# Windowed attention on a quarter of the TensorE array: 64x64 tiles, 48-partition operand stacks, and masks added by matmul

## The chip, the cores and the metric

The kernel runs on one core of one Trainium2 chip. The metric is the device time of one execution in microseconds. All times of the profile come from one profiled execution of the kernel before.

## The reference, cut to what matters

The input is x of 8 sequences, each 1024 positions by 256 features. A layer norm gives `xn`; then a transformer block with sliding-window attention and a gelu MLP, and an eight-expert layer that picks one expert for each position, are both applied to `xn` and added to x. The part that changes is the attention:

```
B, S, D, H, W, HD = (2, 1024, 256, 16, 64, 16)
scores = einsum('bnqhd,bnkhd->bhnqk', q, kc) * scale     # kc: own block of 64 keys and both neighbours
band = |i + W - j| <= W ; mask = band & valid            # invalid keys lie outside the sequence
scores = where(mask, scores, -1e9)
attn = softmax(scores); out = einsum('bhnqk,bnkhd->bnqhd', attn, vc)
```

So each block of 64 queries sees 192 keys: of the middle 64 all, of the left and the right 64 those inside the band.

## The kernel before, in words

**Loop.** The eight sequences are the turns of one loop, b = 0 to 7. Before it stands a prologue that loads and splits the weights and does the first part of sequence 0. Turn b does the attention of sequence b, its output projection (`b_stage`, L1186), the projections of sequence b+1 (`c2_stage`, L1055), and then the MLP of sequence b (`d_stage`, L1254) woven with the first scores and the expert layer of sequence b+1. The last turn has no b+1 parts. Each engine has its own program with the same order of stages, written out by hand; semaphores tie them together, and an engine that waits holds all that is queued behind on it.

**Projections and stacks.** `c2_stage` makes q and k of the next sequence in eight units. ScalarE writes the rounded part (`qk_h`, L918), VectorE the remainder (`qk_l`, L626). A score is computed in f16 as high x high plus high x low plus low x high. The three products lie in one contraction: for each head, 16 partitions of each of the three parts stand above each other, 48 partitions in all. SyncE builds these stacks (`stacks`, L269): it stores high and low parts to DRAM (`pair_dram`, L274; four stores of 512 KB), waits, and loads them back in 12 loads of 256 KB, each onto 16 partitions of `q_s` or `k_s` (L284), first q, then k. Two copies `q_s<-q_s` (L288) come last. `k_s` holds two heads above each other at partitions 0 and 64. `q_s` has a slot for each of the 16 heads with zeros where the other head's partitions are, so that a matmul over all 128 partitions picks one head.

**Scores twice.** The attention needs the row maxima before the exponentials. A step works on four heads (one group g of four) and one tile of 128 positions; there are 32 steps.
- `scores` (L1118) computes queries x keys in blocks of 64x192, eight matmuls a step into the two PSUM banks SB. VectorE adds the mask and takes the maxima (`maxima`, L703, four instructions a step at L713, each with a read of its accumulator).
- After each group `max_cols` transposes the maxima (L1139), VectorE scales them (L720), and SyncE writes them through DRAM into a row of `q_s` (L325, L331), where they join the contraction as one more row against a constant row of `k_s`.
- `scores_t` (L1142) computes keys x queries, 128x256, four matmuls a step into the two banks TB; ScalarE takes the exponentials (`exps`, L933, two of 512 columns a step at L943) into `prob`.
- GpSimd zeroes what lies outside the band (`band`, L435, two instructions a step at L440 and L445); in the steps 22 to 27 (`SHARED`) VectorE does the second one (L727).
- `values` (L1158) multiplies `prob` by v in f32 on four 32-column tiles, into the banks OB. `heads_out` (L946) copies them away.

**Order.** Scores run ahead of the exponentials by LEAD = 14 steps: six after units 5, 7, 9, 11, 13 and 15 of the 16 W1 units of the turn before (`W1_STEPS`), eight with its W2 tiles, and the 18 left in steps 1 to 18 of the attention. In those steps TensorE does half of `scores_t`, half of `scores`, the other halves, and then `values` of two steps before (`turn`, L1278). Steps 19 to 31 have `scores_t` and `values` alone. SB[0] also serves the ranks of the expert layer; the banks MB (6 and 7) serve the transposes.

**W1 units.** A unit (`w1_unit`, L1228) is six matmuls of 512 columns. ScalarE does the gelu (L989) and its rounded copy (L955), VectorE the remainder (`gelu_low`, L790). TB has two banks and `g32` two slots, so TensorE can run two units ahead of VectorE.

**GpSimd.** In its order: 32 times `band`; `residual` (L451, L453) of b+1; an inverse root (L386); `residual_attn` (L459); `fetch` (eight gathers at L490, then the add at L495); `send` (eight scatters of the expert layer's rows, L476); `residual_mlp` (L466, L468), which VectorE waits for before the first W2 tile. SyncE: the maxima's rows, loads of x and the residual, `store_res`, `stacks`, then the expert layer's tiles (`sorted_tiles`, L304), whose first load waits for the scatters.

Of the kernel before, what the change touches and what calls it, by code (L numbers as in the profile page):

```python
# [30 lines left out]
P = 128  # L31
W = 64
# [22 lines left out]
def build(nc, x, Wq, bq_c, Wk, bk_c, Wv, bv, Wo, bo, g1_c, b1, W1, c1_c, W2, c2, g2, b2, gateT, expT, b1_c, g1_row, out):  # L55
# [11 lines left out]
    SHARED = range(22, 28)  # L67
    XN_AT = 23
    WIN = 3 * W
    QW = 4 * W  # L70
# [9 lines left out]
    pair_dram = nc.dram_tensor("pair_dram", (2, 4, P, S), F16, kind="Internal").ap()  # L80
# [6 lines left out]
    assert len(W1_STEPS) + T == LEAD  # L87

# [4 lines left out]
    with ExitStack() as ctx:  # L93
# [8 lines left out]
        mask = sb("mask", [P, 3, WIN], BF16)  # L102
# [25 lines left out]
        pool2 = sb("pool2", [P, 3 * 4 * QW], F32)  # L128
        q_s = sb("q_s", [P, H, S + 2 * W], F16)
# [15 lines left out]
        keep = sb("keep", [P, 2 * W], BF16)  # L145
# [11 lines left out]
        prob = pool2[:, :].rearrange("p (s h q) -> p s h q", s=3, h=4)  # L157
# [15 lines left out]
        SB, TB, OB, MB = bank[0:2], bank[2:4], bank[4:6], bank[6:8]  # L173
# [27 lines left out]
        NSTACK = 2 * 2 * 3 + 2  # L201
        stack = count("stack", 16 * NSTACK)
        pair_st = count("pair_st", 16 * 4)
# [4 lines left out]
        ST_ps, ex_done, masked, pv = (count(n, k) for n, k in (("ST_ps", 2 * STEPS), ("exp_done", 2 * STEPS), ("masked", 2 * STEPS - len(SHARED)), ("pv", STEPS)))  # L208
        masked_v = count("masked_v", len(SHARED))
        oT_ev = count("oT_ev", 2 * G)  # L210
# [25 lines left out]
        def _(sp):  # L236
# [31 lines left out]

            def stacks(b):  # L269

                for qk in range(2):
                    for half, (src, done) in enumerate(((qk_h, qk_hi), (qk_l, qk_lo))):
                        sp.wait_ge(done.sem, done.at(b, 4 * qk + 4))
                        sp.dma_start(pair_dram[half, 2 * qk:2 * qk + 2].rearrange("o p s -> p o s"),  # L274
                                     src[:, 2 * qk:2 * qk + 2, :]).then_inc(pair_st.sem, 16)
                    sp.wait_ge(pair_st.sem, pair_st.at(b, 32 * (qk + 1)))

                    for a in range(2):
                        for slot in range(3):
                            low = slot == (1 if qk else 2)  # L280
                            src = pair_dram[int(low), 2 * qk:2 * qk + 2].rearrange("c (j a d) s -> a d (c j) s", a=2, d=HD)[a]
                            r = W * a + HD * slot
                            dst = k_s[r:r + HD, :, W:W + S] if qk else q_s[r:r + HD, a:H:2, W:W + S]
                            sp.dma_start(dst, src).then_inc(stack.sem, 16)  # L284

                for a in range(2):
                    r = W * a + 3 * HD
                    sp.dma_start(q_s[r:r + 1, a:H:2, W:W + S], q_s[r:r + 1, 1 - a:H:2, W:W + S]).then_inc(stack.sem, 16)  # L288
# [38 lines left out]
            def max_rows_in(b, g):  # L327
                sp.wait_ge(mx_st.sem, mx_st.at(b, 16 * (g + 1)))
                for a in range(2):
                    r = W * a + 3 * HD  # L330
                    sp.dma_start(q_s[r:r + 1, 4 * g + a:4 * g + 4:2, W:W + S],  # L331
                                 max_dram[g:g + 1, a::2, :]).then_inc(mrow.sem, 16)
# [40 lines left out]
        def _(pool):  # L373
# [29 lines left out]
            step(nc.gpsimd.memset(mask[:, :, :], 0.0))  # L403
# [7 lines left out]

            for a in range(2):
                part = mask[W * a:W * a + W, :, :]
                step(nc.gpsimd.affine_select(out=part, in_=part, compare_op=ALU.is_ge, fill=NEG, base=0,
                                             pattern=[[0, 3], [1, WIN]], channel_multiplier=-1))
                step(nc.gpsimd.affine_select(out=part, in_=part, compare_op=ALU.is_ge, fill=NEG, base=2 * W,
# [18 lines left out]
            def band(b, k):  # L435
# [6 lines left out]
                if k in SHARED:  # L442
                    return
# [917 lines left out]
```

## Time and profile before

| | us |
|---|---|
| time, median of 3 runs | 1560.16 (1558.44 to 1561.64) |
| span of the profiled execution | 1553.1 |
| TensorE matmul busy | 1240.9 (80%) |
| VectorE busy | 1071.5 (69%) |
| ScalarE busy | 739.8 (48%) |
| GpSimd busy | 739.9 (48%) |
| mean granted TensorE clock | 0.913 of 2.4 GHz |

The span runs from the first to the last instruction of the profiled execution; the time of a run holds a few microseconds more around it, here 7.1 between this span and the median. An engine's busy time counts overlapping instructions once. Weight loads of TensorE are a row of their own (PEld), since they run beside matmuls. In the profile a wait is told as "engine line waited for: us, times, longest". In a row of the timeline the bracket gives the idle time before the instruction and what ended it.

### The profile page before, as it was taken

The page shows a single profiled execution, that of the slowest core. Times are in us where ns is not written, and L with a number is a line of the kernel's source. Part 1 is how long each engine was busy: PE and PEld are TensorE (multiplying, and loading weights), DVE is VectorE, ACT ScalarE, POOL GpSimd, SP SyncE. Part 2 cuts the span into 40 slices and gives each one's busy share as a digit, 9 for nine tenths or more (in the row PEclk, how much of TensorE's full clock was granted, in tenths as well). Part 3 has the DMA queues.
Part 4 walks back from the last instruction along what each step waited for, and adds up shares of the span by engine and source line. Part 5 has one row for each costly group of instructions (what it writes and reads, how often), then busy time and mean ns, then how long its engine had stood idle before and what let it go on. Part 6 is the DMA issues. An engine that isn't in the chain of part 4 may idle for free.

```text
span 1553.1 us, 34323 instructions
## 1 busy us (share of the span) xinstructions
PE 1240.9 (80%) x10696; PEld 714.8 (46%) x10696; DVE 1071.5 (69%) x3743; ACT 739.8 (48%) x1356; POOL 739.9 (48%) x749
## 2 busy tenths in 40 slices
PE   0648885999678985999859997689858898599967
PEld 0424452735346353654527454373535535265435
DVE  8656775777757775867757677576766676587565
ACT  1305744366543744447443565426544374445642
POOL 6443745156531766037550474406752177504661
PEclk9959997999989997989979899798988899799979
DMA  7463056220733119130462206422082212912010
GB/s 237 92 139 118 3 117 122 76 92 29 144 79 100 57 69 166 50 112 13 108 131 69 99 8 145 91 83 83 33 156 75 88 57 74 162 48 94 2 28 28
DMA packets 89647, 135.00 MB, mean 87 GB/s; under 512 B 10209, under 2 KB 62305, under 8 KB 87393
## 3 DMA queue, kind: packets, MB, share of 16 engines
q1 hardware_dynamic: 83328, 115.91, 30.0%
q0 software_dynamic: 6144, 16.79, 4.4%
q8 instruction: 107, 1.75, 0.5%
q14 instruction: 68, 0.55, 0.1%
HBM read 74.47 MB, written 59.90 MB: 87 GB/s over the span
## 4 chain that ended last, share of the span: by engine, by line
PE 49%; DMA 17%; issue 11%; POOL 8%; DVE 8%; SPq 3%; ACT 3%; DVEq 0%; POOLq 0%; ACTq 0%
DMA pair_dram<-pool 9%; PE bank L1132 8%; PE bank L1035 8%; PE bank L1154 8%; PE bank L1036 7%; PE bank L1038 7%; PE bank L1181 6%; DMA q_s<-q_s 5%; DVE xn L604 2%; SPq L284 2%; DMA ys_dram<-xn 2%; PE bank L1102 2%; POOL x_sb L453 2%; POOL x_sb L451 2%; POOL rs L386 2%
## 5 line engine op out<-in xcount | busy, mean ns | idle before, releaser
L713 DVE CUSTOM_DVE_ANT_0 bank<-bank,mask 128x192 f32<-128x192 f32 x1024 | 337.3, 388 | 199.1 <-PE bank L1132 195.1
L943 ACT ACTIVATE pool<-bank 128x512 f32<-128x512 f32 x512 | 293.0, 597 | 118.9 <-PE bank L1154 113.2
L1132 PE MATMUL bank<-k_s,q_s 128*64 128x192 f16 x2048 | 175.3, 269 | 144.1 <-DMA q_s<-q_s 141.2
L440 POOL TENSOR_SCALAR_AFFINE_SELECT pool<-pool 128x512 f32<-128x512 f32 x256 | 172.2, 675 | 194.1 <-ACT pool L943 193.4
L1154 PE MATMUL bank<-q_s,k_s 128*128 128x256 f16 x1024 | 199.3, 290 | 28.7 <-issue 21.3
L389 POOL TENSOR_TENSOR rs<-ve,neghalf 128x1 f32<-128x1 f32 x64 | 36.9, 577 | 384.8 <-DVE ve L776 384.8
L1132 PEld LDWEIGHTS bank<-k_s,q_s 128*64 128x64 f16 x2048 | 77.8, 113 | 250.1 <-issue 226.9
L1181 PE MATMUL bank<-pool,v_a 128*32 128x256 f32 (+2 forms) x2560 | 161.1, 345 | 19.9 <-DVE pool L727 8.6
L989 ACT ACTIVATE pool<-bank,c1c 128x512 f32<-128x512 f32 x128 | 87.8, 686 | 169.5 <-PE bank L1038 132.5
L790 DVE TENSOR_TENSOR pool<-pool 128x512 f16<-128x512 f32 x128 | 106.7, 839 | 63.3 <-ACT pool L955 62.2
L713 DVE DVE_READ_ACCUMULATOR2_ANT m_sb<- 128x1 f32 x1024 | 144.6, 141 | 0.3
L931 ACT ACTIVATE xn<-bank 128x256 f32<-128x256 f32 x120 | 46.1, 384 | 202.6 <-PE bank L1038 195.0
L1154 PEld LDWEIGHTS bank<-q_s,k_s 128*128 128x128 f16 x1024 | 67.0, 100 | 144.5 <-ACT pool L943 76.4
L445 POOL TENSOR_SCALAR_AFFINE_SELECT pool<-pool 128x512 f32<-128x512 f32 x208 | 132.5, 637 | 0.0
L1036 PE MATMUL bank<-w_l,pool 128*128 128x256 f16 x512 | 115.3, 273 | 0.0
L1035 PE MATMUL bank<-w_h,pool 128*128 128x256 f16 x512 | 115.2, 273 | 0.0
L1035 PE MATMUL bank<-tr_h,w_h 128*128 128x512 f16 x256 | 105.3, 411 | 11.5 <-ACT pool L989 11.5
L1036 PE MATMUL bank<-tr_l,w_h 128*128 128x512 f16 x256 | 104.2, 407 | 0.0
L918 ACT ACTIVATE pool<-bank,bqk 128x512 f16<-128x512 f32 x64 | 44.0, 687 | 93.1 <-PE bank L1038 93.1
L1181 PEld LDWEIGHTS bank<-pool,v_a 128*32 128x32 f32 x2560 | 53.0, 110 | 71.8 <-issue 27.2
L955 ACT ACTIVATE pool<-pool 128x512 f16<-128x512 f32 x128 | 80.6, 630 | 4.5
L1038 PE MATMUL bank<-tr_h,w_l 128*128 128x512 f16 x256 | 80.8, 399 | 0.0
(149 smaller groups left out, 2511.1 us busy)
## 6 DMA issues: line engine op xcount, KB each, us to landing
pair_dram<-pool SPq DMA_DIRECT2D x32, 512.0 KB, 7.6
xn<-xs_dram SPq DMA_DIRECT2D x40, 384.0 KB, 3.7
ys_dram<-xn SPq DMA_DIRECT2D x120, 128.0 KB, 1.7
q_s<-pair_dram SPq DMA_DIRECT2D x48, 256.0 KB
k_s<-pair_dram SPq DMA_DIRECT2D x48, 256.0 KB
x_sb<-in_L_attn_x SPq DMA_DIRECT2D x8, 1024.0 KB, 5.7
res_dram<-x_sb SPq DMA_DIRECT2D x8, 1024.0 KB, 4.8
res_r<-res_dram SPq DMA_DIRECT2D x8, 1024.0 KB, 7.4
```

Source lines behind the costliest of these rows:

```text
L440: nc.gpsimd.affine_select(out=p, in_=p, compare_op=ALU.is_ge, fill=0.0, base=0, pattern=[[0, 4], [1, 2 * W]], channel_multiplier=-1).then_ ...
L445: nc.gpsimd.affine_select(out=p, in_=p, compare_op=ALU.is_ge, fill=0.0, base=0, pattern=[[0, 4], [-1, 2 * W]], channel_multiplier=1).then_ ...
L713: ins = nc.vector.tensor_tensor_reduce(out=SB[u % 2][:, i * WIN:i * WIN + WIN], in0=SB[u % 2][:, i * WIN:i * WIN + WIN], in1=mask[:, v, :] ...
L790: nc.vector.tensor_tensor(gL[hf][:, c, :], g32[:, u % 2, :], gH[hf][:, c, :], ALU.subtract).then_inc(g_lo.sem, 1)
L943: nc.scalar.activation(prob[:, (k + 2) % 3, 2 * pu:2 * pu + 2, :], TB[u % 2][:, :].rearrange("p (h q) -> p h q", h=2), ACT.Exp, scale=EXP_ ...
L989: nc.scalar.activation(g32[:, u % 2, :], TB[u % 2][:, :], ACT.Gelu_apprx_tanh, bias=c1c[:, c:c + 1], scale=1.0 / WS).then_inc(gel.sem, 1)
L1035: nc.tensor.matmul(dst, lh[c], rh[c], start=start and c == 0, stop=False)
L1036: nc.tensor.matmul(dst, lh[c], rl[c], start=False, stop=False)
L1038: mm = nc.tensor.matmul(dst, ll[c], rh[c], start=False, stop=stop and c == n - 1)
L1132: mm = nc.tensor.matmul(SB[u % 2][W * bl:W * bl + W, i * WIN:i * WIN + WIN], q_s[:, h, W + w0:2 * W + w0], k_s[:, h // 2, w0:w0 + WIN], st ...
L1154: mm = nc.tensor.matmul(TB[u % 2][:, i * QW:i * QW + QW], k_s[:, h // 2, W + t * P:W + t * P + P], q_s[:, h, t * P:t * P + QW], start=True ...
L1181: mm = nc.tensor.matmul(OB[hf][32 * hl:32 * hl + 32, a - hf * HALF:z - hf * HALF], v_a[:, t, 4 * g + hl, :], prob[:, (k + 2) % 3, hl, q0:q ...
```

## The change

Six edits go together.
- **Stacks.** The columns of Wq, bq, Wk and bk are permuted on the host so that in a projection's output partition d * 8 + head holds feature d of a head. The stores write `pair_dram` in the stack's order, in 12 stores of 256 KB; the loads take a whole stack of 48 partitions for four head slots at once, 8 loads of 384 KB. The projections' units come in the order q and k of heads 0 to 7, then q and k of heads 8 to 15, and SyncE stores unit pair i and then loads pair i-1. `scores` waits at step 0 for the stacks of heads 0 to 7 alone and at step 16 for the others. `q_s` has the form of `k_s`; the `q_s<-q_s` copies go.
- **64x64 tiles.** `scores` and `scores_t` both compute blocks of 64x192 over one head's 48 or 64 partitions, eight matmuls each a step, ordered over both row halves (the parity of the head) and both column halves.
- **Masks by matmul.** Four matmuls more for `scores` and four for `scores_t` a step, each of 256 columns, add -1e30 outside the band by an identity. GpSimd's and VectorE's `band` go, and VectorE's maxima are two plain reductions of 2x192 columns a step.
- **Values.** `values` computes over the 64 keys of a block, on eight 64x32 tiles, the upper and the lower keys of a tile into different banks (OB, and 6 and 7); VectorE adds the two (`heads_sum`, two a group). The exponentials are of 384 columns.
- **Banks.** MB is now SB, so that `max_cols` waits for all scores issued so far, and the next scores (at `MAX_STEPS`) wait for VectorE's copy.
- **Order.** A step issues all of `scores_t`, waiting for both exponentials of the step before, and then all of `scores`, waiting for both maxima of the step before.

```diff
-    SHARED = range(22, 28)
+    MAX_STEPS = [LEAD - T + 3] + [T * g + MAX_AT - 1 + LEAD for g in range(G - 2)]
-        SB, TB, OB, MB = bank[0:2], bank[2:4], bank[4:6], bank[6:8]
+        SB, TB, OB = bank[0:2], bank[2:4], bank[4:6]
+        MB = SB
+        PV = (bank[4:6], bank[6:8])
...
+            def pair_stores(b, i):
+                c, qk = divmod(i, 2)
+                for src, done, slots in ((qk_h, qk_hi, (0, 2 if qk else 1)), (qk_l, qk_lo, (1 if qk else 2,))):
+                    sp.wait_ge(done.sem, done.at(b, 2 * i + 2))
+                    for slot in slots:
+                        sp.dma_start(pair_dram[c, qk, :, :, slot, :, :].rearrange("j a d s -> d (j a) s"),
+                                     src[:, 2 * qk + c, :]).then_inc(pair_st[i % 2].sem, 16)
+            def stack_loads(b, i):
+                c, qk = divmod(i, 2)
+                sp.wait_ge(pair_st[i % 2].sem, pair_st[i % 2].at(b, 48 * (i // 2 + 1)))
+                dst = k_s if qk else q_s
+                for a in range(2):
+                    sp.dma_start(dst[W * a:W * a + KW, 4 * c:4 * c + 4, W:W + S],
+                                 pair_dram[c, qk, :, a, :, :, :].rearrange("j o d s -> (o d) j s")).then_inc(stack[c].sem, 16)
             def stacks(b):
+                pair_stores(b, 0)
+                for i in range(1, 4):
+                    pair_stores(b, i)
+                    stack_loads(b, i - 1)
+                stack_loads(b, 3)
...
             def maxima(b, j):
+                for n, par in enumerate((1, 0)):
+                    dve.wait_ge(S_ps.sem, S_ps.at(b, 2 * j + n + 1))
                     dve.sem_inc(passed, 1)
+                    nc.vector.tensor_reduce(m_sb[:, 4 * g + par:4 * g + 4:2, t],
+                                            SB[par][:, 0:2 * WIN].rearrange("p (h c) -> p h c", h=2), AX.X, ALU.max).then_inc(mx.sem, 1)
+            def heads_sum(b, g, hf):
+                dve.wait_ge(oT_ev.sem, oT_ev.at(b, 2 * g + hf + 1))
+                o = oT[:, g, hf * HALF:hf * HALF + HALF]
+                nc.vector.tensor_tensor(o, PV[1][hf][:, :], o, ALU.add).then_inc(oT_sum.sem, 1)
...
+            def mask_mm(out, n, t, par):
+                r = slice(W * par, W * par + W)
+                band = mask[r, edge(2 * t + n), :, :].unsqueeze(1).broadcast_to([W, 2, 2, W])
+                dst = out[W * n:W * n + W, 0:2 * WIN].rearrange("p (h c k) -> p h c k", h=2, c=3)[:, :, 0::2, :]
+                return nc.tensor.matmul(dst, ident16[r, :], band, start=False, stop=True, skip_group_check=True)
+            def scores(b, j, first=False):
+                for par in (1, 0):
+                    scores_wait(b, j, par, first)
+                t = j % T
+                for i in range(2):
+                    for n in range(2):
+                        for par in (1, 0):
+                            score_mm(SB[par], n, j, par, i)
+                for n in range(2):
+                    for par in (1, 0):
+                        mm = mask_mm(SB[par], n, t, par)
+                        if n == 1:
+                            mm.then_inc(S_ps.sem, 1)
...
             def turn(b, last):
                 for k in range(STEPS + LAG):
                     if k % T == MAX_AT and k < 3 * T:
-                        max_cols(b, k // T + 1)
-                    for pu in range(2):
-                        if k < STEPS:
-                            scores_t(b, k, pu)
-                        if 1 <= k and k - 1 + LEAD < STEPS:
-                            scores(b, k - 1 + LEAD, half=pu)
+                        max_cols(b, k // T + 1, min(k - 1 + LEAD, STEPS))
+                    if k < STEPS:
+                        scores_t(b, k)
+                    if 1 <= k and k - 1 + LEAD < STEPS:
+                        scores(b, k - 1 + LEAD)
```

`scores_wait` waits for `mx.at(b, u - 1)` of both parities before the first matmul, and at `MAX_STEPS` for `mT_ev`. `scores_t` has the same form with q and k exchanged and waits for `ex_done.at(b, 2 * k)`. On GpSimd the inverse root and `residual` of b+1 now come first in the turn.

## Rows read from the trace of the kernel before

**Rows 1.** Waits of the whole run, TensorE's for the stacks: us, times, longest.
```profile
PE bank L1132 <- DMA q_s<-q_s: 141.2, 8, 22.6
```

**Rows 2.** Waits from 560 to 640 us, inside turn 2.
```profile
PE bank L1132 <- DMA q_s<-q_s: 17.1, 1, 17.1
```

**Rows 3.** Timeline of SyncE's issues in turn 1: start us, us, what.
```profile
392.15 5.24 SPq L274 DMA_DIRECT2D pair_dram<-pool  x2
420.11 2.69 SPq L284 DMA_DIRECT2D k_s<-pair_dram  x6
422.84 1.38 SPq L288 DMA_DIRECT2D q_s<-q_s  x2
```

**Rows 4.** Windows of turn 1: busy us of each engine, then PEclk, DMA share, GB/s.
```profile
416.00:418.00 2.00, 1.31 (x7) 0.39 (x4) 2.00 (x1) 0.10 (x1) 2.00 (x1) 1.00 1.00 278
424.00:432.00 8.00, 0.00 (x0) 0.00 (x0) 0.76 (x1) 0.34 (x1) 6.16 (x8) 0.61 1.09 124
435.00:439.00 4.00, 3.68 (x15) 1.55 (x16) 1.37 (x8) 0.11 (x1) 3.92 (x2) 0.50 0.42 148
```

**Rows 5.** Timeline from 413 to 437 us of turn 1, GpSimd and who it holds.
```profile
414.47 4.50 POOL L495 TENSOR_TENSOR res_r<-res_r,x_sb 128x2048 f32<-128x2048 f32 x1 [10.12 <-DMA x_sb<-ys_dram,pos_y]
...
420.97 0.39 PE L1035 MATMUL bank<-tr_h,w_h 128*128 128x512 f16 x1 [3.66 <-ACT pool L989]
...
431.79 4.52 POOL L466 TENSOR_TENSOR pool<-pool,bc 128x2048 f32<-128x2048 f32 x1
...
435.32 0.85 PE L1132 MATMUL bank<-k_s,q_s 128*64 128x192 f16 x8 [12.88 <-DMA q_s<-q_s]
...
436.39 4.51 POOL L468 TENSOR_TENSOR pool<-pool,bc 128x2048 f32<-128x2048 f32 x1
```

**Rows 6.** Timeline of attention step 13 of turn 2, and the next step's start.
```profile
522.68 0.39 PE L1154 MATMUL bank<-q_s,k_s 128*128 128x256 f16 x2
...
523.00 0.36 PE L1132 MATMUL bank<-k_s,q_s 128*64 128x192 f16 x4
...
523.11 1.21 ACT L943 ACTIVATE pool<-bank 128x512 f32<-128x512 f32 x2 [0.58 <-PE bank L1154]
...
523.29 0.39 PE L1154 MATMUL bank<-q_s,k_s 128*128 128x256 f16 x2
...
523.55 0.37 DVE L713 CUSTOM_DVE_ANT_0 bank<-bank,mask 128x192 f32<-128x192 f32 x1 [0.42 <-PE bank L1132]
...
523.90 0.64 PE L1181 MATMUL bank<-pool,v_a 128*32 128x192 f32 x16
...
524.47 0.39 PE L1154 MATMUL bank<-q_s,k_s 128*128 128x256 f16 x2
```

**Rows 7.** Costliest groups by form: busy us, mean ns, idle before.
```profile
L943 ACT ACTIVATE pool<-bank 128x512 f32<-128x512 f32 x512 | 293.0, 597 | 118.9 <-PE bank L1154 113.2
L1154 PE MATMUL bank<-q_s,k_s 128*128 128x256 f16 x1024 | 199.3, 290 | 28.7 <-issue 21.3 <-ACT pool L943 4.1 <-DMA q_s<-max_dram 1.3
L972 ACT ACTIVATE pool<-bank 128x256 f32<-128x256 f32 x64 | 24.6, 385 | 65.1 <-PE bank L1216 49.8 <-PE bank L1208 15.3
L691 DVE TENSOR_REDUCE tef<-own 128x15 f32<-128x105 f32 x8 | 2.1, 263 | 0.3
L666 DVE TENSOR_REDUCE tiles<-oh 128x8 f32<-128x64 f32 x8 | 1.8, 220 | 0.3
```

**Rows 8.** Timeline of turn 1: steps without scores, first, 28th and last.
```profile
351.81 0.61 PE L1154 MATMUL bank<-q_s,k_s 128*128 128x256 f16 x4
...
365.38 1.09 ACT L943 ACTIVATE pool<-bank 128x512 f32<-128x512 f32 x2 [0.51 <-PE bank L1154]
...
369.61 0.61 PE L1154 MATMUL bank<-q_s,k_s 128*128 128x256 f16 x4
```

**Rows 9.** Timeline of turn 1: VectorE's copy of the maxima.
```profile
353.25 0.28 DVE L720 TENSOR_SCALAR mT<-bank 32x128 f16<-32x128 f32 x1 [0.88 <-PE bank L1139]
```

**Rows 10.** Window inside those steps, columns as in rows 4.
```profile
362.00:365.00 3.00, 1.70 (x21) 0.68 (x22) 3.00 (x8) 2.35 (x5) 0.65 (x1) 1.00 0.02 5
```

More of the change, by code:

```diff
@@ L267, in load_x @@
                 sp.dma_start(x_sb[:, :, :], x_v[b]).then_inc(x_in.sem, 16)
-            def stacks(b):
[L271 to L288, printed above, removed]
@@ L497, in turn @@
             def turn(b, last):
-                for k in range(STEPS):
-                    band(b, k)
-                    if k == XN_AT - 1 and not last:
-                        rstd(b + 1, 0, ve0, rs0)
                 if not last:
+                    rstd(b + 1, 0, ve0, rs0)
                     residual(b + 1)
@@ L838, in turn @@
                         xn_low(b + 1, k - (STEPS - 4))
+                heads_sum(b, G - 1, 1)
                 b_stage(b)
@@ L1116, in sorted_expert, with edge, score_mm @@
                 mm.then_inc(y_ps.sem, 1)
-            def scores(b, j, first=False, half=None):
+            def edge(n):
+                return 0 if n == 0 else 2 if n == 2 * T - 1 else 1
+            def score_mm(out, n, j, par, i):
                 g, t = divmod(j, T)
-                if j == 0 and not half:
-                    pe.wait_ge(route.sem, route.at(b, 6))
-                    pe.wait_ge(stack.sem, stack.at(b, 16 * NSTACK))
-                for pu in range(2) if half is None else (half,):
-                    u = 2 * j + pu
-                    if not first or u >= 2:
-                        pe.wait_ge(mx.sem, mx.at(b, u - 1))
-                    for i in range(2):
-                        h = 4 * g + 2 * pu + i
-                        for bl in range(2):
-                            w0 = (2 * t + bl) * W
-                            mm = nc.tensor.matmul(SB[u % 2][W * bl:W * bl + W, i * WIN:i * WIN + WIN],
-                                                  q_s[:, h, W + w0:2 * W + w0], k_s[:, h // 2, w0:w0 + WIN],
-                                                  start=True, stop=True)
-                    mm.then_inc(S_ps.sem, 1)
@@ new lines, in values @@
+                    pe.sem_inc(passed, 1)
+                pieces = []
+                for a in range(2):
+                    blk = 2 * t + a
+                    for hf in range(2):
+                        lo, hi = max(blk - 1, T * hf, 0), min(blk + 2, T * hf + T)
+                        if lo < hi:
+                            pieces.append((a, hf, blk, lo, hi))
+                for hl in range(4):
+                    for a, hf, blk, lo, hi in pieces:
+                        first = blk in (0, 1) if hf == 0 else blk in (T - 1, T)
+                        last = blk in (T - 1, T) if hf == 0 else blk in (2 * T - 2, 2 * T - 1)
+                        c = (lo - blk + 1) * W
+                        r = slice(W * a, W * a + W)
+                        mm = nc.tensor.matmul(PV[a][hf][32 * hl:32 * hl + 32, (lo - T * hf) * W:(hi - T * hf) * W],
+                                              v_a[r, t, 4 * g + hl, :], prob[r, (k + 2) % 3, hl, c:c + (hi - lo) * W],
```

194 lines of the change are left out of this document (99 added, 95 removed).

## The prediction

> **What bounds the kernel now.** I read the waits of the whole run first, then the same list turn by turn, then SyncE's issues and the windows around the largest wait, then single steps of the attention. The largest wait of TensorE that nothing else covers is the one for the operand stacks: 141.2 us in 8 waits [rows 1]. The longest, 22.6 us, is the prologue's; the seven in the turns sum to 118.6 us, each like the 17.1 us of turn 2 [rows 2]. It stands at the first scores of the next sequence, in the middle of the W1 units. SyncE issues the k loads only at 420.11 us and the copies behind them at 422.84 us [rows 3], and TensorE does nothing in that window, while the queues move 124 GB/s at full share [rows 4]. After the wait the clock is at 0.5, which is 1.2 GHz, for about 4 us [rows 4].
>
> In the attention each step with scores takes 524.47 - 522.68 = 1.79 us, and TensorE follows itself without a gap [rows 6]. Of that only part is columns. Two `scores_t` matmuls of 256 columns take 0.21 us at 2.4 GHz, and the next group starts 0.32 us after them; the four of `scores`, two tiles side by side, take 0.16 us and hold 0.29 us. So a change of tile form costs about 0.12 us, five times a step. `values` holds 0.57 us, 0.45 us without its change. The 12 steps without scores take (369.61 - 351.81) / 12 = 1.48 us [rows 8].
>
> **The change part by part.**
>
> *TensorE in the attention.* If all four 64x64 tiles run side by side, `scores_t` is two waves of 192 columns and one of 256, 0.27 us, `scores` the same, `values` 0.45 x 192/256 = 0.34 us, and two changes of form are left: 1.12 us in place of 1.79 us. TensorE stops being the bound. What is late next is the way through the banks, since `scores` now waits for both maxima of the step before and `scores_t` for both exponentials.
>
> *Loop of the maxima.* From the first `scores` matmul to VectorE's start 0.55 us pass now [rows 6]. The mask wave starts 0.08 us later than today's last matmul and is 0.03 us longer: 0.66 us. A reduction grows by 43 ns for 41 columns [rows 7], so 384 columns take 220 + 320 x 1.05 = 556 ns. Two in a row should overlap as two exponentials do (1.09 us for two of 0.597 us [rows 8, 7]), so 1.02 us. For the way back I take 0.15 us, between the 0.04 us from TensorE's end to ScalarE's start and the 0.19 us to VectorE's [rows 6]. Sum 1.83 us against 1.79 us: 18 steps cost 0.7 us a turn. The bounds are 1.7 us (return 0.05 us, mask wave free) and 2.07 us (no overlap, and 0.3 us back through the added semaphore instructions).
>
> *Loop of the exponentials.* An exponential of 384 columns is 385 + 128 x 212/256 = 491 ns [rows 7], the pair 0.88 us. From `scores_t` to ScalarE 0.43 us pass now [rows 6], 0.09 us more with the mask wave; with the same 0.15 us back, 1.55 us. That is 0.07 us more than now, over 12 steps 0.8 us a turn. The bounds are 1.45 and 1.75 us.
>
> *The shared banks.* At steps 4 and 12 the transpose of the maxima stands between two scores: 0.29 us for the transpose, as for a matmul of twice its columns [rows 7], 0.19 us to VectorE, 0.28 us for the copy [rows 9]; 0.76 us each, 1.5 us a turn. In the W2 tiles one such wait is left, 0.5 us in seven turns: 3.5 us. It could be nothing, or 0.9 us each.
>
> *Band and sums.* GpSimd's 64 selections a turn ran beside the rest and are worth nothing; where `values` waited for them or for VectorE's share, that is inside the 1.48 us. `heads_sum` fits into VectorE's 0.7 us of waiting in a step. The last one stands ahead of the projection, and the last `values` no longer waits for GpSimd: I take zero for the two together (bounds 0.7 us a turn either way). The attention thus costs 0.7 + 0.8 + 1.5 = 3.0 us a turn, **24 us** over eight, with bounds of -12 and +70 us.
>
> *The stacks.* Stores grow from 2 to 3 MB, loads stay at 3 MB, issues go from 18 to 20, but the first scores need only the first half, and it goes first. In turn 1 the store that waits for the low part of four units is issued by 392.15 + 5.24 = 397.4 us [rows 3]; after the change the low part of two is enough, so I start there. Behind it stand 1.8 MB of stores at up to 278 GB/s, 1.6 MB of loads, 1 MB of gathers. The new loads go to 48 partitions, three times as many as the old; at the old loads' 124 GB/s [rows 4], the slow end, all has landed after 23 us, at 420 us. The wait began at 435.32 - 12.88 = 422.4 us [rows 5]. So the wait goes: **-118.6 us**, with 1 us a turn left for late landings, **+7 us** (bounds 0 and 21). The cold start behind it goes too: at half clock the 3.68 us of matmuls [rows 4] would take some 2.2, so 1.5 us a turn, **-10.5 us**. The prologue's wait I cost at nothing (bound -22.6 us [rows 1]), because its expert tiles then wait for GpSimd's scatters. If the second half is late, sixteen steps cover it; SyncE's later start on the expert tiles is covered as long as the scatters, behind which GpSimd goes on at 431.79 us [rows 5], are what they wait for.
>
> The Trainium skill (SBUF — State Buffer, Door 1: The DMA port swizzle) says that 16 partitions reach four of 16 ports and 48 reach eight. The full DMA share at 124 GB/s agrees with that for the old loads; by the rule the new ones would be faster and the 7 us would be nothing.
>
> *What the wait had hidden.* GpSimd's long adds hold VectorE where both of its inputs are in SBUF: during the one of 4.50 us at 414.47 us TensorE waited 3.66 us for the gelu behind VectorE [rows 5]. The two of `residual_mlp`, from 431.79 to 440.90 us, lie in the stack wait now. Without it they fall into the W1 units: 2 x 3.7 us in seven turns, **+52 us** (bounds 0 and 63). That add stood ahead of the stack wait in turn 1, 3.66 + 12.88 us together, and inside it in turn 2, whose one wait of 17.1 us is as long [rows 5, 2]. I take the six other turns like turn 2: 6 x 3.7 = **+22 us** (bounds 0 and 27).
>
> **Sum.** -118.6 - 10.5 + 7 + 52 + 22 + 24 + 3.5 = -20.6 us. The profiled span of 1553.1 us becomes 1532.5; this execution stands 7.1 us below the median of the runs, so the forecast is **1540 us**.
>
> **The rivals.**
>
> *The way through the banks is dearer (slower).* Place: the 30 steps of each attention. If the reductions don't overlap and the semaphores cost 0.1 us more each way, the loops are 2.07 and 1.75 us: 18 x 0.24 + 12 x 0.2 = 6.7 us a turn, 54 us, 1594 us. It decides once the steps are 0.09 us longer than I count (20.6 / 8 / 30). For it: today each half step has its own bank and waits for the one two before, and that slack goes. Against it: both engines get less work. Chance 0.14.
>
> The Trainium skill (TensorEngine Tiling (Array Packing), PSUM Bottleneck) warns that tiling speeds up the array and not the emptying of the banks. That is this rival's side; by the rule alone nothing of the 0.67 us on TensorE arrives, as in my sum.
>
> *The row halves take turns.* Then the change doesn't do what it says: two waves become four, 0.27 us more in each loop, 30 x 0.27 x 8 = 65 us, 1605 us. No row shows two row halves; the column halves do overlap [rows 6]. Chance 0.09.
>
> *The clock falls.* TensorE is busy half of each step without scores. At the half clock these are 0.27 us longer, 12 x 0.27 x 8 = 26 us, 1566 us. Against it: with 1.70 busy of 3.00 us the granted clock stayed at 1.00, 2.4 GHz [rows 10]. Chance 0.05.
>
> *The stack wait stays,* because six megabytes in small pieces take longer. Then the adds stay hidden as well: 1560 + 24 + 3.5 = 1588 us. Chance 0.04.
>
> *The adds don't bite.* With the gathers landing earlier or the adds in gaps of VectorE, the 74 us are in part free: between 1466 and 1515 us. Chance 0.13.
>
> **How the numbers follow.** My forecast has 0.55, its own range from its inner bounds is 1510 to 1572. Two in ten may fall outside: I leave out the lower half of the last rival and the worst of the row halves, and take 1497 to 1598 us. About 0.2%, 3 us, is what can be told from no change. Of my forecast's chance 0.49 is faster, 0.04 is the same, 0.02 slower; the last rival is faster, the others slower with 0.02 of them the same. Faster 0.62, the same 0.06, slower 0.32.
>
> **What would show it.** In the profile after: no wait of TensorE for a stack over 3 us inside a turn; two waits of 3 to 4 us for gelu during L466 and L468's successors, and the first expert tile about 7 us earlier in the turn; steps with scores of 1.83 us with TensorE idle for 0.7 us, without scores 1.55 us; reductions of about 556 ns; the first matmuls of `scores` on all four tiles within some 20 ns. I am wrong if these steps are over 1.92 us, if a second matmul on the other row half starts a wave late, if the granted clock in the attention is 0.5, or if the adds run without holding VectorE.

## The result, and the profile after

The changed kernel takes 1593.4 us (median; 1592.2 to 1594.9) where the kernel before takes 1559.3: a ratio of 1.0226 (95% interval 1.0202 to 1.025). The forecast was 1540 us; the changed kernel is 2.3% slower than the kernel before. Its profiled span is 1592.2 us, 39.1 us over the span before.

The first fence has lines of the page: busy time, the instruction queue, and the costliest groups (busy us, mean ns, idle before them).

```profile
PE 1217.2 (76%) x15816; PEld 737.0 (46%) x15816; DVE 1016.4 (64%) x2223; ACT 672.5 (42%) x1356; POOL 440.3 (28%) x286
...
q8 instruction: 147, 2.41, 0.7%
...
L702 DVE TENSOR_REDUCE m_sb<-bank 128x2 f32<-128x384 f32 x512 | 262.5, 553 | 205.2 <-PE bank L1135 202.8
L932 ACT ACTIVATE pool<-bank 128x384 f32<-128x384 f32 x512 | 223.2, 488 | 251.2 <-PE bank L1135 251.2
L777 DVE TENSOR_TENSOR pool<-pool 128x512 f16<-128x512 f32 x128 | 152.1, 1196 | 84.4 <-ACT pool L946 66.8
L1228 PE MATMUL bank<-pool,v_a 64*32 64x192 f32 (+2 forms) x4608 | 170.3, 336 | 23.4 <-issue 22.4
```

The instruction queue of the kernel before stood at less:

```profile
q8 instruction: 107, 1.75, 0.5%
```

A reduction takes 553 ns and an exponential 488 ns, as counted (556 and 491). No row of the waits names a stack any more; the 141.2 us of [rows 1] are gone. New are a mean of 1196 ns for `gelu_low` (L777), and 22.4 us for which `values` (L1228) waited for nothing that the profile shows. The next fence is the timeline of one step and the start of the next, the counterpart of [rows 6].

```profile
530.84 0.36 PE L1119 MATMUL bank<-k_s,q_s 48*64 48x192 f16 x8 [0.44 <-DVE m_sb L702]
...
531.00 0.31 PE L1135 MATMUL bank<-mask,ident 64*64 64x256 bf16 x4
...
531.25 0.59 PE L1228 MATMUL bank<-pool,v_a 64*32 64x192 f32 x24
531.46 1.02 DVE L702 TENSOR_REDUCE m_sb<-bank 128x2 f32<-128x384 f32 x2 [0.77 <-PE bank L1135]
...
532.28 0.87 ACT L932 ACTIVATE pool<-bank 128x384 f32<-128x384 f32 x2 [0.97 <-PE bank L1135]
...
532.63 0.56 PE L1119 MATMUL bank<-k_s,q_s 48*64 48x192 f16 x8 [0.39 <-DVE m_sb L702]
```

In the `scores` at 530.84 us four matmuls start within 0.01 us of each other, the next four 0.11 us later, and the masks 0.16 us after the first: so four tiles do run side by side, the two row halves among them. From one `scores` to the next 532.63 - 530.84 = 1.79 us pass, as before the change. Now read step 8 of the same turn:

```profile
518.88 0.54 PE L1228 MATMUL bank<-pool,v_a 64*32 64x192 f32 x11
519.10 1.02 DVE L702 TENSOR_REDUCE m_sb<-bank 128x2 f32<-128x384 f32 x2 [0.17 <-PE bank L1135]
521.45 0.14 PEld L1228 LDWEIGHTS bank<-pool,v_a 64*32 64x32 f32 x5 [2.41 <-issue]
521.46 0.52 PE L1228 MATMUL bank<-pool,v_a 64*32 64x192 f32 x5 [2.04 <-issue]
```

TensorE stops in the middle of `values`, after 11 of 16 matmuls, though their operands were there for the first. Such a step takes 4.0 to 5.7 us in turns 1 to 6.

The difference by stages, from the first exponential of each turn, the first transpose of `b_stage`, the first gelu, and the first expert tile in the two timelines; sums over all turns, us:

| stage | before | after | difference | forecast |
|---|---|---|---|---|
| prologue | 136.9 | 132.8 | -4.1 | 0 |
| attention | 442.5 | 498.7 | +56.2 | +24 |
| `b_stage`, `c2_stage` | 298.6 | 315.4 | +16.8 | 0 |
| W1 units to the first expert tile | 301.9 | 267.3 | -34.6 | -48.1 |
| W2 tiles, end of the last turn | 373.2 | 378.1 | +4.9 | +3.5 |

They sum to the spans' difference of 39.1 us but for rounding. (The -48.1 are -118.6 - 10.5 + 7 + 52 + 22.) Against the forecast of -20.6 us the attention is off by 32 us, `b_stage` with `c2_stage` by 17, the W1 stage by 13.5, and the prologue by -4.

### The profile page after: what moved, and what is told of

The parts are those of the page before. It is cut to its first block, busy times and chain, and to the rows that moved or that the text cites. A ratio compares the mean times of both kernels' runs of the same rounds, so it can differ in the third digit from the quotient of the medians.

```text
span 1592.2 us, 42888 instructions
## 1 busy us (share of the span) xinstructions
PE 1217.2 (76%) x15816; PEld 737.0 (46%) x15816; DVE 1016.4 (64%) x2223; ACT 672.5 (42%) x1356; POOL 440.3 (28%) x286
## 3 DMA queue, kind: packets, MB, share of 16 engines
q8 instruction: 147, 2.41, 0.7%
## 4 chain that ended last, share of the span: by engine, by line
issue 65%; POOL 16%; PE 9%; DVE 9%; ACT 1%; POOLq 0%; another core or an unknown queue 0%; DVEq 0%; ACTq 0%
POOL xs_dram L472 4%; PE bank L1029 3%; PE bank L1026 2%; PE bank L1027 2%; POOL pool L464 2%; POOL rs L396 2%; POOL x_sb L449 2%; POOL x_sb L447 2%; POOL pool L462 2%; POOL rs L393 2%; DVE xn L597 1%; DVE oh L637 1%; PE bank L1035 1%; DVE pool L777 1%; DVE pool L619 1%
## 5 line engine op out<-in xcount | busy, mean ns | idle before, releaser
L702 DVE TENSOR_REDUCE m_sb<-bank 128x2 f32<-128x384 f32 x512 | 262.5, 553 | 205.2 <-PE bank L1135 202.8
L932 ACT ACTIVATE pool<-bank 128x384 f32<-128x384 f32 x512 | 223.2, 488 | 251.2 <-PE bank L1135 251.2
L777 DVE TENSOR_TENSOR pool<-pool 128x512 f16<-128x512 f32 x128 | 152.1, 1196 | 84.4 <-ACT pool L946 66.8
L1228 PE MATMUL bank<-pool,v_a 64*32 64x192 f32 (+2 forms) x4608 | 170.3, 336 | 23.4 <-issue 22.4
L1119 PE MATMUL bank<-k_s,q_s 48*64 48x192 f16 x2048 | 105.3, 281 | 98.9 <-DVE m_sb L702 78.6
L1135 PE MATMUL bank<-mask,ident 64*64 64x256 bf16 x2048 | 172.4, 308 | 0.0
L1127 PE MATMUL bank<-q_s,k_s 64*64 64x192 f16 x2048 | 103.4, 281 | 78.0 <-ACT pool L932 48.6
L1119 PEld LDWEIGHTS bank<-k_s,q_s 48*64 48x64 f16 x2048 | 47.2, 113 | 169.5 <-issue 169.2
L1228 PEld LDWEIGHTS bank<-pool,v_a 64*32 64x32 f32 x4608 | 69.5, 111 | 82.8 <-issue 81.5
L472 POOL DMA_INDIRECT xs_dram<-xn,pos x64 | 64.8, 1013 | 55.9 <-DVE pos L677 36.7
```

Source lines behind the costliest of these rows:

```text
L472: nc.gpsimd.indirect_dma_start(out=xs_dram[:, :], out_offset=bass.IndirectOffsetOnAxis(ap=pos[:, t:t + 1], axis=0), in_=xn[:, t, :], in_of ...
L702: nc.vector.tensor_reduce(m_sb[:, 4 * g + par:4 * g + 4:2, t], SB[par][:, 0:2 * WIN].rearrange("p (h c) -> p h c", h=2), AX.X, ALU.max).th ...
L777: nc.vector.tensor_tensor(gL[hf][:, c, :], g32[:, u % 2, :], gH[hf][:, c, :], ALU.subtract).then_inc(g_lo.sem, 1)
L932: nc.scalar.activation(prob[:, (k + 2) % 3, par::2, :], TB[par][:, 0:2 * WIN].rearrange("p (h q) -> p h q", h=2), ACT.Exp, scale=EXP_SCALE ...
L1119: return nc.tensor.matmul(out[W * n:W * n + W, i * WIN:i * WIN + WIN], q_s[r, h, q:q + W], k_s[r, h, q - W:q + 2 * W], start=i == 0, stop= ...
L1127: return nc.tensor.matmul(out[W * n:W * n + W, i * WIN:i * WIN + WIN], k_s[r, h, p:p + W], q_s[r, h, p - W:p + 2 * W], start=i == 0, stop= ...
```

## The experiments

Each ratio is against the kernel before on the same chip, so ratios are compared, 1% being about 15.6 us. The edits are cut to the lines that matter. The stacks alone, the two kernels with GpSimd's operations cut and the pad on TensorE ran on one chip (kernel before: 1560.9 us), the loads moved, the pad on ScalarE and the operations moved on a second (1549.1), the others on a third (1550.9 and 1548.5); the first pair's chip isn't on record (1559.3).

The chips differ in more than that. In the traces of the first chip and in that of the changed kernel ScalarE has waits without a releaser, which the profile puts down to "issue" or "remote" and to no instruction of the program, in the W1 stage and in `c2_stage`. In the changed kernel they are these:

```profile
ACT pool L980 <- remote: 21.8, 7, 5.4
ACT pool L908 <- issue: 10.5, 12, 1.5
```

In the ten traces of the other two chips there is none at these lines, whatever the edit. So a difference of some 1% between runs on different chips can be the chip's.

**The stacks alone.** In the kernel before, `pair_stores`, `stack_loads`, the new order of units and the two waits for halves replace the old ones; the two resets of the maxima's row go behind the first stores. The host doesn't permute Wq and Wk, so the heads' values are mixed up while all work is done.

```
+ dst = k_s[r, 4 * c:4 * c + 4, W:W + S] if qk else q_s[r, 8 * c + a:8 * c + 8:2, W:W + S]
- pe.wait_ge(stack.sem, stack.at(b, 16 * NSTACK))
+ pe.wait_ge(stack[0].sem, stack[0].at(b, 96))
```

> The kernel before with the new stores and loads of the stacks alone (48-partition loads, units in the new order, the first scores wait for the first half); tiles, masks and band as before. Theory A (the stacks give what the prediction counted, and the loss lies in the tiled attention): 1559 - 118.6 - 10.5 + 7 + 74 = about 1511 us, no wait for a stack over 3 us inside a turn, attention steps as before (1.79 us, 12 steps without scores 17.8 to 18.7 us). Theory B (the stacks' own traffic costs what it gains): 1545 us or more, with a wait for a stack left or the W1 stage as long as before.

Measured 0.9799 (0.9772 to 0.9825), 1531 us. No wait for a stack is left, and the attention steps are those of before. So the two halves of the change go opposite ways: the stacks give 2.0%, the tiles cost 1.0226 - 0.9799 = 4.3%, about 66 us. The gain is 31 us, between the 48 of theory A and the 14 or less of theory B.

**GpSimd's operations cut.** Two kernels, the changed one and the stacks alone:

```
- nc.gpsimd.tensor_tensor(n1[:, :, :], n1[:, :, :], bc[:, 4:5, :].broadcast_to([P, T, D]), ALU.mult)
+ nc.gpsimd.tensor_tensor(n1[:, 0, 0:8], n1[:, 0, 0:8], bc[:, 4, 0:8], ALU.mult)
```

> The changed kernel with GpSimd's three long operations in the W1 stage (the add after the fetch and the two of residual_mlp) cut to 8 elements a row; the rest of these sums is left out. Theory C (GpSimd's long operations hold VectorE longer than predicted, about 3 us at the one-hot row and 4.5 us at each of two gelu_low, and the cold clock follows from these waits): 12 us in each of seven turns, 1593 - 84 = about 1509 us. Rival (other work is late next, the scatters or the routing): a gain under 40 us, 1553 us or more.

> The stacks alone, and GpSimd's three long operations cut as well. If the adds bite as predicted, 74 us under the run with the stacks alone: about 1437 us. If the stack wait only hid other late work, less than 30 us under it.

Measured 0.9734 (0.9713 to 0.9754) and 0.9417 (0.9392 to 0.9442): 4.9% and 3.8% less than with the operations, 77 and 60 us where 84 and 74 were expected. In the seven W1 stages it is 63 us (267.3 to 204.2) and 54 us (263.9 to 210.0). The timeline of the changed kernel, turn 2, shows what they do:

```profile
602.83 4.50 POOL L491 TENSOR_TENSOR res_r<-res_r,x_sb 128x2048 f32<-128x2048 f32 x1 [7.69 <-DMA x_sb<-ys_dram,pos_y]
...
604.27 3.14 DVE L637 TENSOR_TENSOR oh<-sc,mx 128x64 f32<-128x64 f32 x1
...
608.66 0.19 PE L1079 MATMUL bank<-oh,before 128*128 128x72 f16 x1 [3.32 <-DVE oh L648]
...
621.13 0.69 ACT L980 ACTIVATE pool<-bank,c1c 128x512 f32<-128x512 f32 x1 [3.83 <-remote]
...
622.51 10.18 DVE L777 TENSOR_TENSOR pool<-pool 128x512 f16<-128x512 f32 x2 [3.55 <-issue]
622.72 4.52 POOL L462 TENSOR_TENSOR pool<-pool,bc 128x2048 f32<-128x2048 f32 x1
...
627.31 4.83 POOL L464 TENSOR_TENSOR pool<-pool,bc 128x2048 f32<-128x2048 f32 x1
...
633.78 0.54 PE L1119 MATMUL bank<-k_s,q_s 48*64 48x192 f16 x8 [6.30 <-DVE m_sb L702]
```

The add after the fetch stretches a VectorE operation of 64 columns to 3.14 us and TensorE waits 3.32 us for the one-hot rows. The other two make two `gelu_low` last 10.18 us, and behind them stands the maximum that frees the bank of the next `scores`: 6.30 us of wait for TensorE, while ScalarE waits 2.55 and 3.56 us ahead of two gelus. So the price comes not as two gelu waits alone, but as a held VectorE with everything behind it.

**The same operations moved.** They are cut by tile and put between GpSimd's operations of the W2 tiles; the sends go first.

```
- residual_mlp(b)
+ for t in range(2): residual_mlp(b, t); residual_y(b, t)
  for t in range(T):
      rstd(b, 2, ve2, rs2, t)
+     if t + 2 < T: residual_mlp(b, t + 2); residual_y(b, t + 2)
```

> The stacks alone, with GpSimd's three long operations of the W1 stage cut into eight tiles each and moved between its tile operations of the W2 stage; the sends go ahead of them. Theory C: VectorE is no longer held in the W1 stage, and in the W2 stage it has slack of 20%: 30 to 60 us under the run with the stacks alone, 1470 to 1500 us. Rival (held by small pieces just the same, or GpSimd's rstd behind them comes late for f_out): within 15 us of 1531.

> The changed kernel with the same cut and move of GpSimd's three operations. Theory C: 40 to 75 us under it, 1518 to 1553 us, and about 50 to 60 us over the run that has the stacks alone with this same cut, since the tiled attention costs the same in both. Rival (the tiled attention only loses against the adds' order): within 25 us of that run.

Measured 0.9147 (0.9117 to 0.9177) with the stacks alone, 1418 us where before takes 1549, and 0.960 (0.9564 to 0.9635) with the whole change. Both gains are over 6%, more than forecast (1470 to 1500 and 1518 to 1553 us) and more than with the operations cut. The W1 stage takes 23.9 and 23.8 us a turn where the kernel before has 43.1; the W2 tiles take some of it back (316.9 to 337.2 us with the whole change). The sends don't explain why moving gives more than cutting: the first starts 5.5 us after the turn's first gelu in both (6.1 to 8.3 us in the changed kernel). In the cut form of the changed kernel ScalarE still waits 61 us ahead of its gelus in seven turns, in the moved form 23, and these runs were on different chips; how much is the chip's is not shown. The tiles' price, measured on one chip here, is as before, 4.5% (72 us by the medians, 50 to 60 expected).

**TensorE's code moved by 128 instructions.**

```
+ for _ in range(128):
+     pe.sem_inc(passed, 1)
  with pe.Fori(0, NB - 1) as b:
```

> The changed kernel with 128 semaphore instructions on TensorE between the prologue and the loop; nothing in the loop differs, but its code stands 128 instructions further on. Theory D (TensorE waits for the next block of its instructions, of which it has 46% more a turn than before): the long step of 4 to 5.7 us, step 8 in turns 1 to 6, moves by one or two steps (some 87 instructions are one step), and those of the last turn move as well; the time may change by up to 15 us either way. Rival (the wait is for data, or for the 2 MB of loads issued two steps earlier): the long step stays step 8, and the time is the same within 3 us.

Measured 1.0365. The first exponential comes at 152.39 instead of 132.81 us, so the 128 instructions put it off by 19.6 us; from there to the end 1459.6 us pass, as in the changed kernel (1459.4). But step 8 is a plain step now (1.8 us), and the long ones are steps 1 (2.9 to 3.4 us in turns 1 to 6), 10 (up to 3.9 us) and 30 (2.9 to 3.1 us in most turns). Two rows of turn 2, TensorE's timeline:

```profile
528.87 0.53 PE L1127 MATMUL bank<-q_s,k_s 64*64 64x192 f16 x8 [2.15 <-issue]
...
548.41 0.36 PE L1119 MATMUL bank<-k_s,q_s 48*64 48x192 f16 x8 [2.19 <-issue]
```

The waits belong to places in the code, and not to one step's data. 2.41 MB in 147 packets is 16 KB each; the queue carried 107 before. Around step 8 of the changed kernel's turn 2 (513 to 521 us) the queues carry one such packet among 2 MB of data (packets, MB, share of 16 engines):

```profile
q1 hardware_dynamic: 1185, 2.07, 74.3%
q8 instruction: 1, 0.02, 0.8%
```

The Trainium skill (Runtime: NRT & Kernel Launch, Instruction fetch mechanics) says that instructions are fetched in blocks of 16 KiB while the block before runs, and that this is mostly hidden. The packet size agrees; that it is hidden holds for most blocks here, but not in step 8, by 2 us.

The trace has the start of each packet of this queue. In turn 2 one starts at 518.93 us, and `values` goes on at 521.46, 2.53 us later. It is so every time: in the attention of the changed kernel 78 such packets start, and the nine waits of TensorE over 1 us for which the profile names nothing (1.1 to 2.8 us, behind the first microsecond of each turn) end 2.3 to 2.9 us after the start of one. With the pad there are 18 such waits, ending 2.2 to 2.7 us after a packet; the attention of the kernel before has 44 packets and no such wait.

**The data beside it moved.** The loads of x and of the residual go behind the second pair of max rows.

```
  max_rows(b, 1)
+ max_rows(b, 2)
  load_x(b + 1); load_res(b)
- for g in range(2, G): max_rows(b, g)
+ max_rows(b, 3)
```

> The changed kernel with the loads of x and of the residual (2 MB) issued after the second pair of max rows, some ten steps later. Theory D1 (a block of TensorE's instructions comes late when its packet meets the data): step 8 of turns 1 to 6 falls from 4.0 to 5.7 us to under 2.5 us, and a long step may appear near steps 17 to 20, where the loads run now; 10 to 18 us less. Theory D2 (the block is late by itself, whatever the queues carry): step 8 stays over 4 us, time the same within 4 us.

Measured 1.0206 (1.0138 to 1.0274). Step 8 is 1.78 to 1.84 us in turns 1 to 6, and step 17, which had 1.8 us, takes 3.6 to 5.3 us; there the loads (issued at 529.85 us in turn 2) now run:

```profile
537.98 0.27 PE L1135 MATMUL bank<-mask,ident 64*64 64x256 bf16 x1 [2.06 <-issue]
```

D1 holds for the place of the wait: the eight waits over 1 us in this attention end 2.3 to 2.7 us after a packet too. But data beside it is not what every such wait needs. In the 3 us ahead of the packet the queues move 368 to 397 GB/s at step 8 of turns 1 to 6, and at most 5 GB/s at step 28 (0.5 to 0.8 us where the profile shows a wait) and at the waits of the last turn (up to 2.0 us). The gain of 10 to 18 us didn't come: the wait moved, the half clock in the attention rose from 135 to 230 us, and the attention is 15 us longer than the changed kernel's (513.9 and 498.7).

**ScalarE's code moved by 64 instructions** (the same edit ahead of ScalarE's loop).

> The changed kernel with 64 semaphore instructions on ScalarE ahead of its loop. Theory D: the wait of 2 to 5 us ahead of the seventh gelu of the W1 stage, for which the profile names no releaser (7 in all, 21.8 us), is ScalarE's own block of instructions and moves to another ScalarE instruction some 64 earlier. Rival (a semaphore, or TensorE's end, is late there): it stays at the seventh gelu. The time stays within 15 us.

Measured 1.0187 (1.0152 to 1.0222), 0.4% under the changed kernel with intervals that overlap. Waits of ScalarE for the gelu, first in the changed kernel, then in this one:

```profile
ACT pool L980 <- PE bank L1029: 60.5, 42, 4.8
ACT pool L980 <- DVE pool L777: 53.1, 18, 3.6
ACT pool L980 <- remote: 21.8, 7, 5.4
```

```profile
ACT pool L980 <- PE bank L1031: 63.2, 44, 5.8
ACT pool L980 <- DVE pool L777: 56.7, 18, 3.6
ACT L932 <- issue: 22.7, 7, 4.1
```

The 21.8 us without a releaser are gone, but that is no answer: this run was on the second chip, and there they are gone in the run with the loads moved too, whose ScalarE code is that of the changed kernel. What the pad did bring is the last line, seven waits of 2.4 to 4.1 us at the table load ahead of a turn's first exponential. No other trace has one over 1 us there. That ScalarE waits for its code there fits; for the 21.8 us the cause stays open. In the changed kernel they end 3.9 to 7.4 us after the last 16 KB packet of the instruction queue, not at one distance from it as TensorE's do.

**Fewer instructions.** Probabilities and v are rounded to fp16, so `values` needs half its matmuls.

```
- v_a = sb("v_a", [P, T, H, VW], F32)
+ v_a = sb("v_a", [P, T, H, VW], F16)
```

> The changed kernel with the probabilities and v kept in fp16 (they are rounded to it): values takes 288 weight loads and 288 matmuls a turn in place of 576 each, so TensorE's instructions fall from about 4350 to 3774 a turn and its time by 0.3 us a step. Theory D (in the attention TensorE waits for its blocks of instructions, not for its columns): the long steps grow rarer or shorter, 15 to 30 us less, 1563 to 1578 us by the first pair of medians. Rival (the steps are set by the way through the shared banks alone): steps stay 1.52 and 1.8 us and the long one stays, under 8 us less.

Measured 1.0354 (1.033 to 1.0379): slower than the changed kernel, by 25 us in the attention (523.9 and 498.7). The idle time ahead of `values` for nothing visible falls from 22.4 us to under 1 us, step 8 is as long as its neighbours in seven of the eight turns, and no wait over 1 us without a releaser is left in the attention:

```profile
L1228 PE MATMUL bank<-pool,v_a 64*32 64x192 f16 (+2 forms) x2304 | 89.8, 308 | 2.8 <-ACT pool L932 1.9
```

But the clock is at 0.5, 1.2 GHz, in nearly the whole attention (windows: busy of each engine, PEclk, DMA share, GB/s; turn 2):

```profile
513.00:543.00 30.00, 24.23 (x458) 11.95 (x454) 16.68 (x33) 12.97 (x30) 0.00 (x0) 0.50 0.21 73
543.00:565.00 22.00, 15.01 (x277) 7.59 (x277) 10.50 (x34) 12.32 (x28) 4.25 (x2) 0.50 0.01 3
```

Its steps take 1.80 us where they take 1.52 at 2.4 GHz, and 2.07 for 1.79. So half of my theory D was right and the forecast of the time wrong: the clock took back more than the waits had cost.

**The clock put back.** Zero-weight matmuls of 512 columns in every `values` (two a step).

```
+ nc.tensor.matmul(PV[1][pieces[-1][1]][0:W, :], q_s[:, 0, 0:W], w1_h[:, 0, 0:512],
+                  start=False, stop=False, skip_group_check=True)
```

> The changed kernel with fp16 probabilities and v, as before, and in every step of values two matmuls of 512 columns with zero weights, which add nothing but keep TensorE at work some 0.4 us more. Theory F (the run without them was slower because the clock fell to 0.5 in the whole attention, where TensorE had too little work): the clock stays at 1.0 in most steps, these take 1.52 and 1.8 us in place of 1.80 and 2.07, and with the long steps gone the time is 25 to 50 us under the run without the fillers, also 10 to 30 us under the changed kernel. Rival (the fp16 form itself is slower, or TensorE's extra work shows): the same or slower.

Measured 1.0196 (1.0144 to 1.0248), 1.6% under the run without them, though TensorE does more. In the second part of turn 2's attention:

```profile
545.00:568.00 23.00, 22.09 (x360) 10.04 (x359) 12.91 (x38) 14.67 (x34) 6.34 (x3) 1.00 0.01 3
```

Half clock in the attention: 82 us instead of 490. A long step is back (step 9, 3.1 to 4.3 us in six of turns 0 to 6), and with it most of what the clock gave.

**The order of halves.** The change's order undone: `scores_t` of one parity, `scores` of one parity, then the others.

```
+ for half in range(2):
+     scores_t(b, k, half)
+     scores(b, k - 1 + LEAD, only=1 - half)
```

> The changed kernel with the order of halves of before: transposed scores of one parity, scores of one parity, then the other two, each waiting for its own bank alone. Two of the four tiles run at a time, so TensorE needs some 0.3 us more a step. Theory E (the order of the change, all transposed scores and then all scores, makes each loop wait for both banks): steps without scores fall from 1.52 to about 1.2 us, those with scores from 1.78 to about 1.6 us, 30 to 55 us less in all if the blocks of instructions allow it. Theory D alone (instructions set the pace): steps 8 and 28 stay long, and less than 15 us are gained.

Measured 1.0158 (1.0112 to 1.0204), 0.7% under the changed kernel, the intervals touching, and on another chip; the attention is 7 us shorter (491.7 and 498.7). A plain step without scores takes 1.13 us, one with scores 1.35 to 1.6: the loops through the banks do shorten by up to 0.4 us. But steps of 2 to 3.5 us now stand between them, step 8 still takes 4.6 to 6.2 us in five turns, and the 12 steps from step 19 on take 19.7 to 22.3 us in turns 0 to 6 instead of 19.0 to 19.5. Both theories had a part, and neither number was met.

**Combinations.** Halves, fp16 and moved operations together; that with one filler a step; and the old tiles with the stacks, fp16 and moved operations.

> The tiled attention with the order of halves, fp16 probabilities and v, and GpSimd's operations in tiles. If order and instruction count were all that the tiles lost by, it comes within 15 us of the old attention with the same edits (about 1375 us). If not, it stays 40 us or more above it.

> Order of halves, fp16 values and GpSimd's operations in tiles, with one filler of 512 columns a step. Theory F: the half clock in the attention (350 of 437 us) goes, and 10 to 30 us with it. Rival: TensorE was the bound there at half clock because of its blocks of instructions; then the long steps come back and under 8 us are gained.

> The stacks alone with GpSimd's operations in tiles, and fp16 probabilities and v. In the old attention TensorE follows itself in the 18 steps with scores (1.79 us), so a values shorter by 0.3 us shows: 18 x 0.3 x 8 = 43 us, about 1375 us where the kernel before takes 1549. Rival (the exponentials are the bound just behind it): under 15 us.

Measured 0.9331 (0.9299 to 0.9363), 0.9348 (0.9321 to 0.9375) and 0.9015 (0.8988 to 0.9042). The filler halved the time at half clock in the attention (354 to 164 us) and gained nothing: the steps 2 to 6 take 2.3 to 3.1 us in most turns. The old tiles stay 3.2% ahead of the best form of the new ones. They gained 1.3% from fp16, 20 of the 43 us expected. At 1395 us (1394 to 1400) this is the fastest version, 10% under the kernel before; with f32 probabilities the fastest is the one of 1418 us.

## Why the prediction was wrong, point by point

**The stack wait** (-118.6 us) went as argued: no row is left of it, late landings cost nothing, and the prologue even gave 4 us. With GpSimd's operations moved the stage takes 23.9 instead of 43.1 us a turn, 135 us less in seven.

**What the wait had hidden** was the right mechanism, but "2 x 3.7 us" was not how it came: the second `gelu_low` is held as well, and so is the maximum behind it, with the bank of the next `scores`. In size the term was a little too large: with the one add that already bit the sum had 78 us, and cutting the operations takes 63 us out of the seven stages. What failed in this stage is a term that wasn't there. By the sum, the stage without the operations is 301.9 - 118.6 - 10.5 + 7 - 4 = 176 us; it takes 204.2 us with them cut. So about 28 us of other waits came in place of the stack's. With the operations moved, on another chip, it takes 166.3 us. In the changed kernel 21.8 us of ScalarE's waits have no releaser; the cause of these is open. The forecast that the first expert tile comes 7 us earlier held in four turns (the stage is 5 to 12 us shorter in turns 0, 1, 5 and 6); in turns 2 to 4 the stage took 42.3 us, as long as before.

**The attention** (+24 us) is where the sum broke, by 32 us. Its parts were right: the row halves don't take turns, steps without scores take 1.52 us (1.55 counted), the steps 13 to 18 with scores 1.72 to 1.99 (1.83), reductions 553 ns (556). The steps that stand out over their neighbours are step 8 in turns 1 to 6 (28.8 us together, 18.0 over 1.8 each), step 28 in seven turns (6.4 over 1.52 each) and four of the last turn (7.3): 31.7 us. The pad, the moved loads and the halved `values` show what they are for step 8, and the pad for step 28 too (it is 1.52 us there in five of seven turns): TensorE runs out of code. The packets say the same, also for the last turn's four, whose waits end 2.6 to 2.9 us after the start of one. That the 31.7 us come so near to the 32 is in part luck: over the eight turns the steps 3, 4 and 11 grew by 15 us as well and the steps 25 to 27 shrank by 8, with only 3 us a turn counted for all but the long steps. The step of the prediction that failed is one that isn't there. It priced each matmul by its columns and its change of form and never counted instructions, though the tiles make 15816 matmuls out of 10696, with as many weight loads. "TensorE stops being the bound" was true for its array and false for its instructions.

**The clock** was a rival at 0.27 us a step with a chance of 0.05. The size was right (0.28), the place was not, and the chance was too small. The rival put it into the 12 steps without scores, and these ran at 2.4 GHz in turns 0 to 6; the half clock lies in the steps 0 to 5 and, in five turns, behind step 8. In all the attention has 135 us of it against 53, and when `values` was halved nearly all. At 0.28 us for 1.8 these 82 us more cost about 13 (an estimate); that lies partly in the first steps of each turn, which the sum had at 1.83 us and which take 2.4, 3.2 and 2.2.

**`b_stage` and `c2_stage`** (+17 us, none counted): the stage takes 316 to 320 us in the four traces of the first chip, with the stacks alone as well, and with GpSimd's operations cut as well. On the other two chips it takes 298 to 309 us in all ten. The longer ones, and they alone, have the waits of ScalarE without a releaser there (10.5 us in the changed kernel, 18.8 with the stacks alone). So this goes with the chip and not with GpSimd's operations; what ends these waits stays open.

**The W2 tiles** came nearly as counted (+4.9 with the end of the last turn for +3.5).

Of the rivals, "the way through the banks is dearer" gave 1594 us and fits the time to 1 us, for the wrong reason: the plain steps were no dearer than counted. The run in halves shows that this way is what a plain step is made of, yet giving it back bought at most 0.7%.

## What to carry to other kernels

Count instructions beside columns: where small tiles multiply matmuls, price the code that the engine must take in, and look at the page's row of the instruction queue. Before you take work from TensorE in a stage that it doesn't bound, ask what its clock will do there. And before removing a wait, move what it hid: the same stacks gave 2.0% with GpSimd's long operations in place and 8.5% with them moved.

## What the runs showed that was not expected

- 128 instructions ahead of a loop moved 2 us waits of TensorE to other steps, and 64 on ScalarE brought 22.7 us of waits to its table loads.
- These waits of TensorE ended 2.2 to 2.9 us after the start of a 16 KB packet of the instruction queue, 35 times of 35 in three traces.
- ScalarE's waits without a releaser in the W1 stage were there in all five traces of the changed kernel and of the first chip and in none of the ten of the other two, whatever the edit.
- Code and data met: with 2 MB of loads moved by some ten steps, the long step moved from step 8 to step 17.
- Less work on TensorE made the kernel slower (1.0226 to 1.0354), and idle columns won 1.6% back.
- 128 semaphore instructions in a row on TensorE put its next work off by 19.6 us, 0.15 us each, as an estimate from one pair of traces.
